# A row's norm shared out anew between VectorE and ScalarE, first tile ahead of the seventh row's choice, last expert split in quarters

## The reference, cut to what matters

```python
x = x + layernorm(attn(layernorm(x)))        # attn: a long convolution, and inside it
    r = u + conv(u) + u * D                  #   u is the normed input
    out = (r - mean(r)) * rsqrt(var(r) + 1e-5) * ln_w + ln_b
x = x + layernorm(ffn(layernorm(x)))         # ffn: a mixture of 8 experts, 2 a token
    z = (u - mean(u)) * rsqrt(var(u) + 1e-5) * g + b
    w = top-2 of softmax(z @ rW + rb), renormed
    mixed = sum over the 2 experts of w * (gelu(z @ W1[e] + b1[e]) @ W2[e] + b2[e])
    out = u + mixed
```

## Time and profile before

| | us |
|---|---|
| median of 3 runs | 555.94 (555.14 to 557.07) |
| the profiled execution | 554.49 |
| its span, first to last instruction | 552.7 |
| TensorE busy | 446.5 (81%) |
| VectorE busy | 438.0 (79%) |
| ScalarE busy | 376.4 (68%) |
| GpSimd busy | 262.7 (48%) |

### The profile page before, as it was taken

How to read it: one execution, slowest core, us unless ns; L and a number is a source line. 1 busy time by engine, 2 the same in 40 slices (tenths; PEclk the granted TensorE clock), 3 DMA queues, 4 the chain that set the end, 5 groups by cost and what they waited for, 6 DMA issues and landing times.

```text
span 552.7 us, 11601 instructions
## 1 busy us (share of the span) xinstructions
PE 446.5 (81%) x2730; PEld 385.8 (70%) x2730; DVE 438.0 (79%) x1423; ACT 376.4 (68%) x928; POOL 262.7 (48%) x194
## 2 busy tenths in 40 slices
PE   0196899967999996587978999999999999999200
PEld 0045888856888885446867897999999999999200
DVE  6999795999898988775887776877777777777185
ACT  5992864455667565884656676777777777777266
POOL 0000359545467877375155534444354444445446
PEclk9998999999999996897989999999999999999755
DMA  6302830032223574398146465545454467645495
GB/s 153 154 1 71 336 127 1 0 133 78 100 92 133 175 231 159 122 337 280 40 109 144 82 121 139 82 79 79 71 85 79 78 110 157 119 78 68 85 376 228
DMA packets 48190, 70.34 MB, mean 127 GB/s; under 512 B 7680, under 2 KB 37248, under 8 KB 47744
## 3 DMA queue, kind: packets, MB, share of 16 engines
q1 hardware_dynamic: 34832, 51.82, 29.1%
q0 software_dynamic: 13296, 17.80, 19.3%
HBM read 37.90 MB, written 31.70 MB: 126 GB/s over the span
## 4 chain that ended last, share of the span: by engine, by line
PE 45%; DVE 25%; ACT 13%; issue 6%; DMA 6%; SPq 2%; POOL 2%; DVEq 1%; ACTq 0%; another core or an unknown queue 0%; POOLq 0%
PE psum L1518 15%; PE psum L1542 13%; PE psum L1528 4%; DMA y_rows<-yw,row_of 3%; PE psum L1438 3%; PE psum L1502 2%; ACT acc L735 2%; DVE ws L958 2%; DVE st L763 2%; PE psum L1396 2%; ACT dump L674 2%; PE psum L1458 2%; DVE o L1170 1%; ACT ws L611 1%; PE psum L1409 1%
## 5 line engine op out<-in xcount | busy, mean ns | idle before, releaser
L1343 POOL DMA_INDIRECT y_rows<-yw,row_of x71 | 110.6, 1558 | 140.3 <-SPq L405 74.7
L1518 PE MATMUL psum<-ws,z_hl 128*128 x426 | 119.3, 416 | 12.6 <-DVE ws L958 5.6
L1542 PE MATMUL psum<-ws,h_hl 128*128 x852 | 116.5, 286 | 0.6 <-DVE h_hl L1124 0.6
L1542 PEld LDWEIGHTS psum<-ws,h_hl 128*128 128x128 f32 x852 | 104.1, 189 | 0.8 <-issue 0.8
L1518 PEld LDWEIGHTS psum<-ws,z_hl 128*128 128x128 f32 x426 | 76.2, 192 | 28.0 <-issue 14.9
L1299 POOL DMA_INDIRECT z_rows<-zn,pos x64 | 70.4, 1099 | 26.2 <-issue 17.6
L656 ACT ACTIVATE hg<-hb 128x512 f32<-128x512 f32 x71 | 44.9, 632 | 31.7 <-DVE hb L1118 26.0
L1438 PE MATMUL psum<-yf,it 128*128 128x256 f32 x256 | 60.8, 394 | 2.6 <-DVE r L1144 2.6
L619 ACT ACTIVATE z_f<-psum,gb 128x128 f32<-128x128 f32 x142 | 57.1, 452 | 6.6 <-PE psum L1502 2.7
L1409 PE MATMUL psum<-pm,ft 128*128 128x256 f32 x256 | 58.2, 382 | 0.4 <-DVE tmp L944 0.4
L649 ACT CAST h_hl<-psum 128x512 fp32r<-128x512 f32 x71 | 41.5, 585 | 24.9 <-PE psum L1528 23.2
(11 more groups left out here) (223 smaller groups left out, 826.0 us busy)
## 6 DMA issues: line engine op xcount, KB each, us to landing
z_in<-z_rows SPq DMA_DIRECT2D x71, 129.5 KB
w_raw<-in_dram SPq DMA_DIRECT2D x16, 512.0 KB, 5.7
xs<-in_dram SPq DMA_DIRECT2D x8, 512.0 KB, 5.5
x_dram<-xs SPq DMA_DIRECT2D x8, 512.0 KB
y_rows<-zn SPq DMA_DIRECT2D x8, 512.0 KB, 3.3
yr<-y_rows SPq DMA_DIRECT2D x8, 512.0 KB, 7.4
out_dram<-acc SPq DMA_DIRECT2D x6, 512.0 KB, 2.7
b1r<-in_dram SPq DMA_DIRECT2D x8, 256.0 KB
```

The source lines that it names most:

```text
L1343: pool.indirect_dma_start(y_rows, bass.IndirectOffsetOnAxis(ap=row_of[:, t:t + 1], axis=0), yw[t % 6][:, :], None, compute_op=ALU.add).the ...
L1518: last = TE.matmul(ps_h[q], z_hl[q][:, a, k], w_at(e, c, k * F, F), start=n == 0, stop=n == 5)
L1542: last = TE.matmul(ps_y[q], h_hl[q][:, a, k], w_at(e, c, 1024 + k * H, H), start=n == 0, stop=n == 11)
```

## The change

Three things are changed.

1. **The norm of r.** The variance moves from VectorE to ScalarE and the scaling from ScalarE to VectorE. VectorE forms r with its sum in four fused operations, takes the negative mean (`r_mean`), and forms (r + mean) * ln_w in four operations (`r_mid`), ahead of `point`. ScalarE sums the squares of r + mean and takes the root. Behind `place`, VectorE takes the reciprocal and forms o * rs + ln_b with its sum.
2. **The end of step 8.** VectorE takes row(0) and the split of expert 6 ahead of the choice of row 6 (the seventh), and bias(0) ahead of its place. TensorE takes transposes(1), four spins and the first layer of tile 0 ahead of the rank of row 6. ScalarE scales tile 1 ahead of the last `renormalise`.
3. **Expert 7** is split in quarters: ScalarE at tiles 4 to 7, VectorE at tiles 16, 19, 22 and 25. TensorE waits for it ahead of tile 32 instead of 14.

```diff
@@ ScalarE, step(n)
                 if cur.live:
+                    act.wait_ge(sem("r_mean"), cur.b + 1)
+                    for k in range(4):
+                        last = nc.scalar.activation(dump[:, k], r[:, k], ACT.Square, bias=mv[2][:, k, 0:1],
+                                                    accum_out=mv[2][:, k, 1:2])
+                    last.then_inc(sem("var2"), 1)
                     sigma(cur, 2)
-                    act.wait_ge(sem("st_r"), cur.b + 1)
-                    for k in range(4):
-                        last = nc.scalar.activation(r[:, k], r[:, k], ACT.Identity, bias=rs[:, 2, 4 + k:5 + k],
-                                                    scale=rs[:, 2, k:k + 1])
-                    last.then_inc(sem("r_norm"), 1)
...
                     nc.scalar.activation(wt[5][:, :], eps[:, 0:1], ACT.Gelu)
+                    scaled(1)
                     renormalise(cur)
-                    scaled(1)
...
-                if i == 3:
-                    split_high(E - 1)
+                if i in LAST_HIGH:
+                    j = LAST_HIGH.index(i)
+                    act.wait_ge(sem(f"in_w{E - 1}"), 32)
+                    nc.scalar.copy(ws[:, E - 1, 0, 512 * j:512 * j + 512],
+                                   w_raw[E - 1][:, 512 * j:512 * j + 512]).then_inc(sem("w7_high"), 1)
@@ VectorE, step(n)
-                    V.tensor_tensor(r[:, 0:2], c, s_sb[:, :, :], ALU.add)
-                    V.tensor_tensor(r[:, 2:4], c, s_sb[:, :, :], ALU.subtract).then_inc(sem("r_ready"), 1)
+                    for k in range(4):
+                        last = V.scalar_tensor_tensor(r[:, k], c[:, k % 2], 1.0, s_sb[:, k % 2], ALU.mult,
+                                                      ALU.add if k < 2 else ALU.subtract, accum_out=st[:, 2, 0, k:k + 1])
+                    last.then_inc(sem("r_ready"), 1)
                     dve.wait_ge(sem("r_ready"), cur.b + 1)
-                    stats(lambda k: r[:, k], 2)
+                    V.tensor_scalar(mv[2][:, :, 0], st[:, 2, 0, 0:4], -1.0 / H, None, ALU.mult).then_inc(sem("r_mean"), 1)
                     if n < B:
                         if tail.live:
                             scales_x1(tail)
                         if last_tail.live:
                             find(last_tail)
-                    do(inverse(cur, 2))
-                    V.scalar_tensor_tensor(rs[:, 2, 4:8], mv[2][:, :, 0], -1.0, rs[:, 2, 0:4], ALU.mult,
-                                           ALU.mult).then_inc(sem("st_r"), 1)
+                    dve.wait_ge(sem("r_mean"), cur.b + 1)
+                    for k in range(4):
+                        last = V.scalar_tensor_tensor(o[:, k], r[:, k], mv[2][:, k, 0:1], lwb[:, 0], ALU.add, ALU.mult)
+                    last.then_inc(sem("r_mid"), 1)
...
-                    dve.wait_ge(sem("r_norm"), cur.b + 1)
-                    do(V.tensor_tensor(o[:, :, :], r[:, :, :], lwb[:, 0].unsqueeze(1).to_broadcast([P, 4, H]), ALU.mult))
+                    inverse(cur, 2).then_inc(sem("st_r"), 1)
+                    dve.wait_ge(sem("st_r"), cur.b + 1)
+                    dve.wait_ge(sem("r_mid"), cur.b + 1)
                     for k in range(4):
-                        last = V.scalar_tensor_tensor(o[:, k], o[:, k], 1.0, lwb[:, 1], ALU.mult, ALU.add,
+                        last = V.scalar_tensor_tensor(o[:, k], o[:, k], rs[:, 2, k:k + 1], lwb[:, 1], ALU.mult, ALU.add,
                                                       accum_out=st[:, 1, 0, k:k + 1])
...
                 if n == B:
-                    choose(tail)
-                    scales_x1(cur)
-                    place(tail)
                     row(0)
                     split_low(6)
+                    scales_x1(cur)
+                    choose(tail)
                     row(1)
+                    bias(0)
+                    place(tail)
@@ VectorE, tiles
-                if i == 7:
-                    split_low(E - 1)
+                if i in LAST_LOW:
+                    last_low(LAST_LOW.index(i))
@@ TensorE
-                if t in (0, FIRST):
-                    pe.wait_ge(sem("w_low"), E - 1 + (t == FIRST))
+                if t == 0:
+                    pe.wait_ge(sem("w_low"), E - 1)
+                if t == B * T // P:
+                    pe.wait_ge(sem("w7_low"), 4)
...
                 if n == B:
-                    spin(2, 0)
+                    transposes(1)
+                    spin(4, 0)
+                    first_layer(0)
                     rank(tail)
-                    transposes(1)
-                    first_layer(0)
+LAST_HIGH = (4, 5, 6, 7)
+LAST_LOW = (16, 19, 22, 25)
```

More of the change, by code:

```diff
@@ L958, in split_low, with last_low @@
                 V.tensor_tensor(ws[:, e, 1], w_raw[e][:, :], ws[:, e, 0].bitcast(F32), ALU.subtract).then_inc(sem("w_low"), 1)
+            def last_low(j):
+                dve.wait_ge(sem("w7_high"), j + 1)
+                at_ = slice(512 * j, 512 * j + 512)
+                V.tensor_tensor(ws[:, E - 1, 1, at_], w_raw[E - 1][:, at_], ws[:, E - 1, 0, at_].bitcast(F32),
+                                ALU.subtract).then_inc(sem("w7_low"), 1)
             def choose(row):
@@ L1215, in _ @@
                 step(n)
-            bias(0)
             final = Row(B - 1, 0)
```

2 lines of the change are left out of this document (1 added, 1 removed).

## The result

| | before | after |
|---|---|---|
| median | 555.64 us (4 runs, 555.14 to 557.07) | 562.18 us (4 runs, 559.47 to 565.9) |
| ratio | | 1.0108, 95% interval 1.006 to 1.0156 |
| profiled execution / span | 554.49 / 552.7 | 559.47 / 557.7 |
| TensorE busy | 446.5 | 452.7 |
| VectorE busy | 438.0 | 434.2 |

The forecast was 553.9, range 549.6 to 556.8. VectorE does have 3.8 us less work, as meant, and yet the kernel is slower. TensorE is busy 6.2 us more: 1.6 us are the two more spins of part 2 (3.60 us for 1.96), the rest is work at half clock.

A forecast was written before the change was run, and what follows sets the result against it. TensorE bounds the kernel, so gains count only where it waits, before 345 us. Norm -1.2, end of rows -1.0, quarters +0.2 sum to -2.0 us: 553.9 against the median 555.94, range 549.6 to 556.8.

The forecast's parts named there:

- Part 1, its length: VectorE's norm in each row: mask about 0.5 us sooner after r, 1.2 us less VectorE work per row.
- Nothing is paid there: ScalarE in the norm: four Square replace four Identity, about 2 us both, started earlier and wanted only after place; no cost.
- Part 1, its place: Row stage: VectorE operations with two SBUF inputs wait for GpSimd in rows 0, 2 and 5; rows sum to -1.2 us.
- Part 2: End of the rows: tile 0 five us earlier, its 5.60 us wait becoming 4.4 at transposes(2) on z_in(2); -1.0 us.
- Half clock may lift within it: After the wait for z_in(2): full clock may return during tile 1's start, range -0.1 to -2.0 us, -1.0 taken.
- their reader comes after 303. Nothing.: Row 6's eight scatters, moved from 247.71 to 250.2 us and ending near 261, cost nothing; load 14 reads them later.
- Part 3: Expert 7's quarters: tile 10's 1.51 us gain is waited away at tile 13; +0.2 us, between 0 and 2.4.
- The rivals: Four alternatives: no GpSimd collisions 550.2 (0.15); load fixes tile 1 555.9 (0.22); late load 558.0 (0.11); split counts 552.4 (0.08).
- a late z_in(2): Tile 1's start: the load lands at 256.6 us, transposes(2) delays the first layer; +2.1 us, 558.0, chance 0.11.
- The chance of 0.11 for slower: Whole kernel: probability given to a slower result, all from z_in(2) landing at 256.6 us, 558.0 us.

The follow-up runs named there:

- e5: Kernel before with only the new norm of r, its four o moved ahead of x1's scales; ratio to before 1.0082.
- e6: Kernel before with only the new norm of r, its four o moved behind the mask; ratio to before 1.0056.
- e7: Kernel before with only the new norm of r, its four o moved behind the mask and the first products; ratio to before 1.0062.
- e8: Kernel before with only the new norm of r, GpSimd's folds of rows 6 and 7 one row later; ratio to before 1.0078.
- e10: Changed kernel with expert 7's weight load moved behind the loads of tiles 4 and 5; ratio to before 1.0106.
- e14: Kernel before with row 5's scatters after row 7's x1 and row 6's in pairs between the tiles; ratio to before 1.0034.
- e2: Kernel before with only the new end of step 8 (tile 0 ahead of row 6's choice and rank, four spins); 554.74 us, ratio 1.0014.
- e13: Changed kernel with row 6's eight scatters in four pairs ahead of the y scatters of tiles 0 to 3; ratio to before 1.0066.
- e3: Kernel before with only expert 7's split in quarters; 553.99 us, ratio to before 1.0013.

## Why the prediction was wrong

1. **Part 1, its length: this step failed.** It said "the mask comes about 0.5 us sooner after r (0.2 to 0.8)"; it came 0.57 later. Removed were 3.06 + 0.30 us (3.44 were counted). Added were 1.67 (r and mean, counted 1.6), 1.59 (four o, counted 1.45) and 0.64 of a wait that the step had not: the sum took scales_x1 as work and forgot that its reciprocal reads ScalarE's root, ready 2.3 us after r. The two statistics passes had been its cover. This is the account of the ranks of rows 1, 2 and 4: 0.5 sooner was counted for each, and each lost 0.57 to 0.62. e5, which covers the wait with the o, has the mask at 5.26 again and loses 0.17 at most there; e6 and e7 show that even with the wait the norm wins up to row 4 if the o don't stand ahead of the mask. "Nothing is paid there", on ScalarE, overlooked the root, though it is right of the four Square.
2. **Part 1, its place: right, but for the operation struck.** Row 0's o ended at 103.0, as said ("near 103"), by the mean's 4.50 us, not by the o's. Behind r of row 2 the collision ended 2.46 us after r started (said: 2.4), behind r of row 5 3.06 (said: 3.3), and the rank there lost 0.87 (said: 0.7); only the mean took the blow that was meant for L954. Removing row 0's collision (e8) moved it elsewhere and gained nothing by row 4.
3. **The clock in the rows was not in the sum at all.** The earlier trace rows were read as slack that a better mask could only shrink. Behind two of these waits, grown from 2.7 to 3.4 and from 1.15 to 2.0, stood half clock, 3.4 of the 6.0 us. The forecast had read half clock behind the 5.60 us wait of part 2, and did not ask for it in the rows, where each wait behind the mask grew. Both of the two grew by the collision on the mean, not by the root, which was ready before the struck mean ended (192.12 and 192.90 us in row 3); and the first is in part chance, as e10 (3.37 us, full clock) and e14 (2.72, half clock) show.
4. **Part 2: mechanism right, but for the clock.** By itself (e2) the wait of 5.60 turned into one of 2.8 at transposes(2), not 4.4, since z_in(2) went out at 248.75 in that execution. Counted from the rank of row 5, tile 0 came 4.3 us sooner ("some five") and tile 1 1.6 (1.0 was taken). "Half clock may lift within it" failed: it lasted to 263 us and took more than that, tile 3 stood 3.1 later by the same count. In the changed kernel the 4 us wait did not come, since the rows were 6 us late and z_in(2) was there; and "their reader comes after 303. Nothing." missed that the moved chain of scatters costs others than its reader: 5.6 us at tile 3, gone in e13's one trace. That the chain alone is the cause is not shown.
5. **Part 3: right.** Tile 10's 1.51 came back at z_in, TensorE waited once, 0.43 us, between 326 and 370 us, where VectorE takes the quarters, and e3's times show no difference. VectorE's load of registers stayed as in the earlier trace rows, 28.8 us of idle instead of 26.9, with two of the quarters in that window:

```profile
L1116 DVE CAST z_hl<-z_f 128x256 fp32r<-128x256 f32 x48 | 14.7, 305 | 28.8 <-PE psum L1537 27.1 <-issue 1.1 <-ACT z_f L619 0.5
```

The rivals had the loss only as a late z_in(2); none had the norm slower. The chance of 0.11 for slower stood on the wrong mechanism. By the sum, the rank of row 4 was to come 1.2 us sooner; it came 5.9 later, of which 3.4 are half clock, 0.9 row 3's collision and the rest, less 0.1 at row 0, the wait for the root.

## What to carry to other kernels

When a step is made shorter, go through what stands behind it and ask of each operand when it is ready: time that work took may have been the cover of another engine's result, and a sum over one engine's instructions doesn't see it. Work that nobody waits for belongs behind what the bounding engine waits for: with the same four operations ahead of the mask part 1 was 6.3 us behind by the rank of row 4 (3.4 of it half clock), with them behind it 1.2 us ahead. Count each wait of TensorE that grows past what it was with the clock behind it, and each gain ahead of a fixed load as lent until that load has been shown to move.
